# The experts' result rows are scattered by GpSimd to their tokens' rows, layer 3 loads them with plain DMAs, and layer 3's first four units run in another order

## The reference

```python
# layer 2, z = WKV mix of x
scores = softmax(z @ W_gate.T)
topk_w, topk_i = top_k(scores, 2);  topk_w = topk_w / sum(topk_w)
eo[t, e] = (silu(z @ gate_proj[e]) * (z @ up_proj[e])) @ down_proj[e]      # 8 experts, hidden 256
x = x + z + sum_k topk_w[t, k] * eo[t, topk_i[t, k]]
# layer 3, z = WKV mix of x (it gates a ratio of scans with sigmoid(x))
z = hadamard(z * SU_ug)
h = silu(z @ W_gate.T * s_g) * (z @ W_up.T * s_u)                            # hidden 2048
x = x + hadamard(h * SU_dp) @ W_down.T * s_d
```

## Time and profile before

| | us |
|---|---|
| median of 3 runs | 1692.98 (1691.78 to 1694.21) |
| the profiled execution | 1696.13 |
| its span | 1694.3 |
| PE busy in the span | 1465.3 (86%) |
| DVE, ACT, POOL busy | 1161.0, 991.9, 478.2 |

### The profile page before, as it was taken

One profiled execution on the slowest core, in us unless ns is written; L12 is line 12 of the kernel. 1 busy time (PEld: TensorE's weight loads), 2 busy tenths in 40 slices (PEclk: granted clock), 3 DMA queues, 4 the chain that ended last, 5 costly groups with the idle time before them and its releaser, 6 DMA issues.

```text
span 1694.3 us, 19173 instructions
## 1 busy us (share of the span) xinstructions
PE 1465.3 (86%) x6133; PEld 934.8 (55%) x6166; DVE 1161.0 (69%) x1746; ACT 991.9 (59%) x1313; POOL 478.2 (28%) x442
## 2 busy tenths in 40 slices
PE   5677579998985799996689999658999999999999
PEld 2222234444443456654544444346788888888887
DVE  7899579999996799995777878878332332323323
ACT  5756499999994799996357777756122121212211
POOL 0000133544431222220044544573122231321211
PEclk9898789999997899998789999878999999999999
DMA  7766642212104988874744545662010110100002
GB/s 282 269 203 203 237 147 71 75 63 81 63 29 125 260 218 207 209 179 163 295 142 157 170 166 159 202 222 75 1 38 1 38 38 1 38 9 29 0 10 91
DMA packets 105494, 210.35 MB, mean 124 GB/s; under 512 B 11508, under 2 KB 28404, under 8 KB 101684
## 3 DMA queue, kind: packets, MB, share of 16 engines
q1 hardware_dynamic: 90500, 173.72, 29.9%
q0 software_dynamic: 14896, 35.40, 9.6%
HBM read 140.13 MB, written 52.17 MB: 113 GB/s over the span
## 4 chain that ended last, share of the span: by engine, by line
PE 44%; DVE 3%; POOL 2%; DMA 2%; issue 1%; ACT 1%; SPq 0%; DVEq 0%; ACTq 0%; POOLq 0%
PE ffn_po L2608 10%; PE ffn_pu L2570 9%; PE ffn_pg L2570 9%; PE moe_psum L1949 8%; PE moe_psum L1970 4%; PE moe_psum L1937 1%; PE moe_psum L1888 1%; DMA rows_of_z<-moe_zrow 1%; POOL ffn_wl L1598 0%; PE moe_psum L1960 0%; POOL ffn_wh L1598 0%; POOL up_front L1598 0%; DVE up_front L1684 0%; POOL in_part L1598 0%; DVE rt_hot_block L2245 0%
## 5 line engine op out<-in xcount | busy, mean ns | idle before, releaser
L2673 DVE SCALAR_TENSOR_TENSOR up_front<-ffn_pu,ffn_up_scale,up_front 128x512 f32<-128x512 f32 x64 | 47.8, 750 | 267.9 <-PE ffn_pu L2570 267.9
L2486 ACT ACTIVATE up_front<-ffn_pg,ffn_gate_chunk 128x512 f32<-128x512 f32 x64 | 43.7, 688 | 288.6 <-PE ffn_pg L2570 287.2
L2537 POOL TENSOR_TENSOR ffn_hl<-up_front,ffn_hh 128x512 fp32r<-128x512 f32 x64 | 82.7, 1295 | 389.8 <-ACT ffn_hh L2493 389.7
L2683 DVE SCALAR_TENSOR_TENSOR x<-ffn_po,ffn_out_scale,x 128x512 f32<-128x512 f32 x128 | 94.9, 750 | 65.3 <-PE ffn_po L2608 65.3
L2608 PE MATMUL ffn_po<-ffn_hh,ffn_wh 128*128 128x512 f32 x256 | 101.1, 395 | 4.0 <-DVE x L2683 4.0
L2570 PE MATMUL ffn_pu<-zhi,ffn_wh 128*128 128x512 f32 x256 | 101.2, 395 | 0.0
L2570 PE MATMUL ffn_pu<-zhi,ffn_wl 128*128 128x512 f32 x256 | 100.7, 393 | 0.0
L2608 PE MATMUL ffn_po<-ffn_hh,ffn_wl 128*128 128x512 f32 x256 | 100.5, 393 | 0.0
L2608 PE MATMUL ffn_po<-ffn_hl,ffn_wh 128*128 128x512 f32 x256 | 100.1, 391 | 0.0
L2570 PE MATMUL ffn_pu<-zlo,ffn_wh 128*128 128x512 f32 x256 | 99.9, 390 | 0.0
L966 POOL TENSOR_SCALAR l_rr<-l_ss 128x1 f32<-128x1 f32 x32 | 16.8, 526 | 272.6 <-ACT l_junk L878 207.5
(11 more groups left out here) (371 smaller groups left out, 4069.3 us busy)
## 6 DMA issues: line engine op xcount, KB each, us to landing
wkv_k<-in_fside SPq DMA_DIRECT2D x64, 256.0 KB, 4.5
ratio<-wkv_fn SPq DMA_DIRECT2D x64, 256.0 KB, 3.0
wkv_ek<-exp_k SPq DMA_DIRECT2D x48, 256.0 KB, 3.3
wkv_ekv<-exp_k_times_v SPq DMA_DIRECT2D x48, 256.0 KB, 4.0
expert_out<-moe_eo SPq DMA_DIRECT2D x39, 256.0 KB
up_front<-in_gated SPq DMA_DIRECT2D x8, 1024.0 KB, 4.9
x<-in_x SPq DMA_DIRECT2D x4, 1024.0 KB, 7.8
down_first_a<-in_down_raw SPq DMA_DIRECT2D x16, 256.0 KB, 2.7
```

Source lines behind the costliest of these rows:

```text
L2486: eng.activation(hf[t], p_g[t][:, :], ACT.Silu, scale=scale).then_inc(*E(f"silu{t}").inc)
L2537: eng.tensor_tensor(hl[t][slot % 2][:, :], hf[t], hh[t][slot % 2][:, :].bitcast(F32), ALU.subtract).then_inc(*E(f"hl{t}").inc)
L2673: eng.scalar_tensor_tensor(hf[t], p_u[t][:, :], scale, hf[t], ALU.mult, ALU.mult).then_inc(*E(f"h{t}").inc)
L2683: eng.scalar_tensor_tensor(x[:, o, :], p_o[:, o, :], out_s[:, o:o + 1], x[:, o, :], ALU.mult, ALU.add).then_inc(*E("x").inc)
```

## The change

Every slot's row goes straight to where its token will look for it. `expert_out` now has 2 x 2048 + 1 rows: row 0 takes the rows of empty slots, row 1 + t the first expert's result for token t, row 2049 + t the second's. The token list carries the choice in its sign (token + 1, or -(token + 1)); `take_list` unfolds it with five small VectorE operations into `token_list` and a new `place_list`, and `sources` is gone. GpSimd stores `eo` with an indirect DMA (`scatter`); since several scatters write row 0, each one waits until the one before it has landed. In layer 3 SyncE loads the result rows plain (`load_parts`), between the loads of the ratios; it stores the last two units' ratios only after `load_parts` of batches 0 and 1. VectorE waits for all ratio stores before it starts on batch 0. Two pieces of the first low weights go from VectorE to GpSimd. ScalarE's weighing of batches 2 and 3 is cut in halves and moved, its turned pieces of the second chunk come before `high_h` of unit 3, and TensorE turns batch 3's rows (`next_cols(3)`) right after `gates_of_new(2)`.

```diff
-    def gather(self, eng, i):
+    def load_parts(self, eng, i):
         for t in range(TPB):
             if i >= 2:
                 eng.wait_ge(*(self.weighed(i - 2, t) if i % 2 else self.E("cols_of_y").at(CT * (i - 2) + CT - 1)))
             for k in range(2):
-                at = bass.IndirectOffsetOnAxis(ap=self.c["moe_source"][k][:, i * TPB + t:i * TPB + t + 1], axis=0)
-                eng.indirect_dma_start(self.parts[i % 2][k][t], None, self.d["expert_out"], at).then_inc(*self.gathered[i % 2 * TPB + t].inc)
+                rows = self.d["expert_out"][ds(1 + k * TOK + (i * TPB + t) * P, P), :]
+                eng.dma_start(self.parts[i % 2][k][t], rows).then_inc(*self.gathered[i % 2 * TPB + t].inc)
...
         def _(eng):
+            def scatter(j):
+                eng.wait_ge(*E("eo").at(j))
+                if j >= 1:
+                    eng.wait_ge(*out_sent[(j - 1) % OUTS].at((j - 1) // OUTS))
+                at = bass.IndirectOffsetOnAxis(ap=place_list[:, j:j + 1], axis=0)
+                eng.indirect_dma_start(d["expert_out"], at, eo[j % OUTS][:, :], None).then_inc(*out_sent[j % OUTS].inc)
...
             eng.wait_ge(*E("token_list").at(0))
+            eng.wait_ge(*E("place_list").at(0))
...
             def take_list():
+                link = lambda ins: links(eng, ins, links.n)
                 eng.wait_ge(*E("listed").at(0))
-                eng.tensor_copy(token_list[:, :], p_list).then_inc(*E("token_list").inc)
+                link(eng.tensor_scalar(second_rows[:, :], p_list, -1.0, -1.0, ALU.mult, ALU.add))
+                link(eng.scalar_tensor_tensor(row_of[:, :], p_list, -1.0, second_rows[:, :], ALU.add, ALU.max))
+                eng.tensor_scalar(token_list[:, :], row_of[:, :], 0.0, None, ALU.max).then_inc(*E("token_list").inc)
+                link(eng.tensor_scalar(second_rows[:, :], p_list, 0.0, float(TOK), ALU.is_lt, ALU.mult))
+                eng.scalar_tensor_tensor(place_list[:, :], row_of[:, :], 1.0, second_rows[:, :],
+                                         ALU.add, ALU.add).then_inc(*E("place_list").inc)
...
-            before(eng, "results", "sources")
+            before(eng, "results")
+            inp.load_parts(eng, 0)
+            before(eng, "first_ratio", "newton")
+            inp.load_ratio(eng, 0)
+            inp.load_parts(eng, 1)
+            before(eng, "last_ratios", "ratios")
+            for i in range(1, BATCH):
+                inp.load_ratio(eng, i)
+                if i + 1 < BATCH:
+                    inp.load_parts(eng, i + 1)
...
+            inp.weigh_both(eng, 2, (0, 1))
+            inp.gates(eng, 1)
+            silus(0)
+            inp.weigh_both(eng, 2, (2, 3))
+            inp.z_high(eng, 1)
+            inp.weigh_both(eng, 3, (0, 1))
+            inp.gates(eng, 2)
+            high_hs(0)
+            silus(1)
+            inp.weigh_both(eng, 3, (2, 3))
+            inp.z_high(eng, 2)
+            inp.gates(eng, 3)
+            high_hs(1)
+            high(BATCH, BATCH)
+            silus(2)
+            inp.z_high(eng, 3)
+            high_hs(2)
+            silus(3)
+            high_turned(1, range(PIECES - 1))
+            high_hs(3)
+            high_turned(1, range(PIECES - 1, PIECES))
...
             inp.weigh_second(eng, 0)
+            before(eng, "ratios")
             inp.gated(eng, 0)
```

More of the change, by code:

```diff
@@ L1622, in weigh_both, with add_both @@
                            scale=self.c["moe_weight"][:, i * TPB + t, 1:2]).then_inc(*self.E("second").inc)
-    def add_both(self, eng, i):
-        for t in range(TPB):
+    def add_both(self, eng, i, tiles):
+        for t in tiles:
             y = self.y[i % 2][t]
@@ L2174, in _ @@
                     gather_block(n)
+                for n in block_of(j, 2, 3):
+                    scatter(n)
                 for n in block_of(j, 0, 1):
@@ L2180, in _ @@
                     w.products(eng, u, u % w.slots)
+                for n in block_of(j, 2, 4):
+                    scatter(n)
                 for u in unit(j, 1, 0):
@@ L2312, in _ @@
             take_list()
-            sources()
             for n in range(UNITS):
@@ L2371, in over @@
                     eng.wait_ge(*out_sent[p].at((NB - 1 - p) // OUTS))
+            elif name == "first_ratio":
+                eng.wait_ge(*w.sent[(UNITS - BATCH) % w.slots].at((UNITS - BATCH) // w.slots))
+            elif name == "last_ratios":
+                for u in range(UNITS - 2, UNITS):
+                    w.store(eng, u, u % w.slots)
             elif name == "ratios":
                 w.stored(eng)
-            elif name == "sources":
-                eng.wait_ge(*E("sources").at(0))
+            elif name == "weights":
                 for k in range(2):
@@ L2438, in send_out @@
                         eng.dma_start(d["out"][:, at:at + TIME], c["x"][:, o, b * TIME:(b + 1) * TIME]).then_inc(*out_sent.inc)
-            before(eng, "results", "sources")
+            before(eng, "results")
[8 more added lines that the diff above has]
+                    inp.load_parts(eng, i + 1)
             for j in range(N + 6):
-                if j == 1:
-                    before(eng, "ratios")
-                for i in due(j, 0, BATCH):
-                    inp.load_ratio(eng, i)
                 for i in due(j, 0, N):
@@ L2471, in first_high, with high_turned @@
                 eng.activation(wh[0][:, 2 * GU:], raw[:, 2 * GU:], ACT.Copy).then_inc(*w_hi.inc)
-            def high_turned(m):
-                for n in range(PIECES):
+            def high_turned(m, pieces):
+                for n in pieces:
                     eng.wait_ge(*turned.at(PIECES * m + n))
@@ L2538, in low_h @@
                                       ALU.subtract).then_inc(*E(f"hl{t}").inc)
-            before(eng, "results", "sources")
-            for b in range(BATCH - 1):
-                inp.gather(eng, b)
-            inp.add_both(eng, 2)
-            inp.gather(eng, 3)
+            eng.wait_ge(*w_hi.at(0))
+            for n in range(PIECES, WCOLS // TIME):
+                last = eng.tensor_tensor(piece(wl[0], n), piece(raw, n), piece(wh[0], n).bitcast(F32), ALU.subtract)
+            last.then_inc(*w_lo.inc)
+            inp.add_both(eng, 2, range(TPB))
+            inp.add_both(eng, 3, (0, 1))
             for i in range(N):
@@ L2691, in first_low @@
                                       ALU.subtract).then_inc(*E("first_lo").inc)
-                eng.wait_ge(*w_hi.at(0))
-                for n in range(PIECES, WCOLS // TIME):
-                    last = eng.tensor_tensor(piece(wl[0], n), piece(raw, n), piece(wh[0], n).bitcast(F32), ALU.subtract)
-                last.then_inc(*w_lo.inc)
             before(eng, "results")
@@ L2761, in build @@
             "moe_weight": sb("moe_weight", [P, TILES, 2]),
-            "moe_source": [sb(f"moe_source{k}", [P, TILES], U32) for k in range(2)],
         }
```

94 lines of the change are left out of this document (37 added, 57 removed).

## The result

| | before | after |
|---|---|---|
| median of 4 runs each, us | 1692.38 (1685.48 to 1694.21) | 1714.65 (1711.69 to 1720.49) |
| ratio, 95% interval | | 1.0143 (1.0107 to 1.0178) |
| span of the profiled execution | 1694.3 | 1709.7 |

The account below looks back on a forecast made before the run. TensorE was taken to bound the expert loop and the stretch from 1180 on, with something to win at layer 3's start. 0.8 + 2.8 + 5.8 - 5.7 = +3.7 on 1692.98 gave 1696.7 us, range 1687 to 1709.

Parts of the forecast that it names:

- Step 1: Taking the token list before the first gather: four more chained small operations at 0.2 us, +0.8 us.
- Step 2: Scatters in the expert loop: landing of 3.4 us makes the next turn's gather 0.4 us late, seven turns, +2.8 us.
- the chain of scatters is the bound: Rival, 25%: in the expert loop a landing takes 4.2 us, the loop loses about 13 us, time 1709.
- Step 3: End of the expert loop: the last result lands 7.35 us later, through the chained last scatters.
- Step 4: Batch 0 of layer 3: VectorE waits for the last ratio stores behind 17 loads, 6.9 us later.
- the rival that they don't hold VectorE: Rival, 25%: last ratio stores don't delay layer 3's batch 0, which starts 6.6 us earlier than forecast; time 1690.
- Step 5: Batches 1 to 3 of layer 3: no gather waited for, 1.1 us won back, leaving +5.8.
- Step 6: At `down(2)` in layer 3: TensorE's wait of 3.97 us and 1.73 of slower matmuls go, -5.7 us.

## Why the prediction was wrong

*Step 1, +0.8: right.* From the place matmuls' start to the first gather it took 3.07 us before (844.39 to 847.46) and 3.85 in after.

*Step 2, +2.8: wrong, and this is the step that failed; it came out at 19.5.* The mechanism was as described: the wait for the landing, the first gather of the next turn behind it, late again each turn. The wait, the chain and its cycle were right; the price of a turn was put at 0.4 and measured 2.25:
- The first link. Between scatters 4 and 5 stand unit 0's two additions, and they, not the landing, make it 4.4 us (4.3 in the kernel without the chain); I had put a landing and 0.3 there, 3.7.
- The wake-up. I took 0.3 from a landing to the next scatter; it is 0.75. Over the other two links that is 0.9 us a turn. The trace of before had shown it: its last store lands at 1087.55, and GpSimd's first gather of results, which waits for it, begins 0.82 later.

```profile
1087.67 0.70 issue
1088.37 0.97 POOL up_front L1598
```

- The landing. 3.4 was near the usual one (2.8 to 3.7), but the 13 that stand in the chain of the loop average 3.67, for two of them take 5.1 to 5.2 and one 4.4.
- The gather. I had let it land 3.57 after its issue, a price read from a gather of layer 3. The chain of before has the loop's first gather at 4.31. In after it took 3.40 to 4.74, 4.19 on average, from the issue of a turn's first gather to TensorE's first matmul on its block; the second fence below has the landing of one, and TensorE's row behind another that was issued at 1067.07. So the gather was due by 916.65, not 917.27, and the slack that the prediction put at a tenth or two wasn't there.

```profile
848.85 4.31 DMA moe_zt<-rows_of_z,rt_token_list
```

```profile
1034.68 4.39 DMA moe_zt<-rows_of_z,rt_token_list
...
1071.81 0.66 PE L1926 MATMUL moe_psum<-ident,moe_zt 128*128 128x128 f32 x4 [3.43 <-DMA moe_zt<-rows_of_z,rt_token_list]
```

- The sum of a turn. From scatter 4 to the gather it takes 15.8 us on average over the six turns: 4.35 for the first link, 9.0 for the other two, and 2.46 for the last issue, `num_later` and gaps, which I had put at 3.03. From 902.85 that gives 918.65, 2.0 late a turn; measured 2.25. The formula held, its inputs did not.
- What a wait costs besides itself. Between the first transpose of a block and the last down the traces have the same 702 matmuls: busy 229.4 us before, 234.7 after, at a granted clock of 0.99 and 0.97. 14.0 us are added waits and 5.2 are the same matmuls at the lower clock, a part of the 19.5 that the chain's terms don't name. I had costed no such thing in the loop, though I did so for `down(2)`. That the full clock would give all of the 5.2 back isn't shown: in a turn that the chain bounds, a quicker TensorE may only wait longer.
- `out(37)`, which waits for scatter 34's landing of 6.51, adds 2.75 of these waits. That ScalarE would be held by the buffers of results I had not considered.

That it was the wait, and neither the five issues a turn nor the traffic, is shown by the kernel without the chain, together with the one that has the own rows and keeps the chain; that it acted through the gather, by the kernel with the gathers ahead.

By step 2's formula a landing of 3.57 would also have made this term some 3.6 larger, not "about 1": 0.5 a turn, for seven turns.

The rival "the chain of scatters is the bound", at 25%, named the right bound, but not by its condition, a landing of 4.2. Its link of 4.2 + 0.3 = 4.5 met the measured 4.4 to 4.5 by luck, with a landing too long and a wake-up too short. Its 13 us were short of 19.5, with the gather at 3.57 and nothing for `out(37)` or the lower clock. My error in the odds was to take a slack of a tenth as a reason for a small loss. Where a cycle has no slack, the outcome hangs on the sign of the next tenth, and the loss grows with the number of turns.

*Step 3, +7.35: right in size, 7.4 beyond the loop's slip*, but by other numbers: landings of 3.2 to 3.5 and long gaps instead of 3.4 and 0.3, and the first of 6.51 hidden in part behind `out(37)`.

*Step 4: the wait for the ratios was there* (6.92 us), and the rival that they don't hold VectorE fell. The term was 2.7 short: from the last landing to the first residual it took 18.2, not 15.5. I had let the 17 loads move at 414 GB/s from the start, but SyncE needs 8.9 us to issue them, 0.43 to 0.67 each, and the last store landed 8.75 after its own issue.

*Step 5: the batches won nothing back; they lost 2.3 more.* Residual to residual it took 19.3, 20.6 and 21.6, in sum 61.5 where I had 59.2. At batch 2 the chain goes through ScalarE's new order:

```profile
1170.22 1.28 ACT L2501
...
1172.78 1.22 ACT up_front L1605 x2
1174.00 1.22 ACT in_part L1621 x2
1175.22 0.53 ACT zhi L1655
```

A table load, a silu and four weighings stand ahead of the rounding that TensorE waits for, which I had priced at 1.0 for all batches together. `low(4)` lay over `outer` again, as predicted. The 0.5 that the step gave back for it had no ground in its rows, and didn't come: from batch 3's residual to its first matmul it took 17.85 us, 17.25 before.

*Step 6, -5.7: right*, 5.45 in the two traces (31.36 from the first matmul of batch 3 to the end of `down(2)`, now 25.91), and 5.2 alone on before.

## What to carry to other kernels

Before a wait for a landing is put on an engine, find what is queued behind it, and count the links between two uses of the same resource: each cost the landing and 0.75 us to wake here. Take each price from a row of the same stage: a gather of another stage made the slack look 0.6 larger than it was. If the sum is within a microsecond of the period, assume that it slips, and that it slips every turn. Where the wait is there only because several writers share one scratch row, give each a row of its own and drop the wait: here that took 1.3% away (1.0143 of before became 1.0016). And look for what the change leaves alone: two edits of one to four lines, taking a wait of 4 us and a hold of 6.4 us off the path, were worth 12 to 14 us, while the rebuilt scheme brought nothing.

## What the runs showed of the hardware

- From the landing of a scatter to the issue of the next one that waits for it: 0.75 us on GpSimd, of which 0.50 passes before its queue's next instruction.
- A scatter of 256 KB to distinct rows landed in 2.7 us with little beside it, in 2.8 to 3.5 in the loop; with all 128 slots of a block written to one row it took 3.2 to 3.5. A gather of the same size took 3.4 to 4.7 in the loop. So a scatter was not slower than a gather. For what step 2 took from the Trainium skill, page "DMA: Bandwidth & Descriptors", section "Anatomy of one DMA — SWDGE (gpsimd) path", that HBM's receipt is the heaviest, the landings here show no price.
- The scatter of block 34 took 6.51 us in after and 5.99 to 6.32 in five of the experiments. Layer 3's weight loads are issued 0.8 to 1.2 us before it in after; that this is the reason was not tried.
- A GpSimd operation of 128x3072 held VectorE's 128x512 one for 7.06 us instead of 0.69. The Trainium skill, page "SBUF — State Buffer", section "SBUF: two separate sides", has an exclusive lock on a port pair that VectorE and GpSimd share, held for the whole instruction; the trace agrees (`outer` ended 0.5 us after `low(4)` in after), and the kernel with `low(4)` moved shows the price: 6.2 us of TensorE's time.
- After TensorE's idle time of 2.31 us in the loop (to 915.33) the granted clock from 916 to 920 was 0.57, a mean over its two levels, 1.2 and 2.4 GHz (0.50 and 1.00); after one of 2.38 us two turns later (to 978.60) it stayed 1.00 from 979 to 983. What tells the two apart these traces don't show.

```profile
916.00:920.00 4.00, 4.00 (x6) 1.55 (x6) 2.59 (x4) 0.60 (x1) 3.08 (x4) 0.57 0.68 230
...
979.00:983.00 4.00, 4.00 (x16) 2.04 (x15) 2.79 (x4) 0.60 (x1) 3.09 (x4) 1.00 0.73 245
```
